# Context stage: a transposed copy of x from memory for pairs 4 to 15, the layer norm folded into the values, and deviations moved by SyncE's DMAs

## The chip, the cores and the metric

The kernel runs on one core of a Trainium2 chip. The metric is the device time of one execution in microseconds; the time before the change is the median of three executions, 522.25 us (520.49 to 522.72). Engines are named as in the profile: PE is TensorE's matmul side and PEld its weight loads, DVE is VectorE, ACT is ScalarE, POOL is GpSimd, SP is SyncE, which here only issues DMAs. A row that says SPq is the issue of a DMA.

## The reference

One layer of a perceiver: 64 sequences of 64 tokens of width 256 (x) and a context of 256 rows of width 192 for each sequence. Three residual blocks follow each other. The change touches the first (and one copy in the second).

```python
x = x + cosine(layernorm(x), ctx, Wv, bv, Wt, bt)   # this change
x = x + attention(layernorm(x), ...)                # 16 heads of 16
x = x + experts(layernorm(x), ...)                  # 14 experts, top 1

def cosine(xn, ctx, Wv, bv, Wt, bt):
    v = xn @ Wv.T + bv                              # (64, 64, 128)
    t = ctx @ Wt.T + bt                             # (64, 256, 128)
    dots = einsum('bih,bjh->bij', v, t)             # (64, 64, 256)
    return dots / maximum(norm(v)[:, :, None] * norm(t)[:, None, :], 1e-8)
```

## The kernel before

Tokens lie in SBUF in 32 tiles of 128 (`tok`). The context stage works on 16 pairs of tiles: pair n holds 256 tokens, which are 4 sequences, and the 1024 rows of their context. Three stages follow on the same engines: context (to about 113 us of the span), attention (to about 350 us) and experts. Each engine has its own instruction stream, written out in order by a `context_step`; semaphores (`need(engine, semaphore, count)`) tie them together. `run_steps` unrolls the first and last steps and makes a loop of those between.

What happens to pair n before the change:

- SP issues the load of the context, `ctxT` (768 KB, L324), and of x two pairs further (256 KB, L310). At its step 6 it first issues 12 loads of constants (L316).
- DVE takes mean and variance of x (`bn_stats`, `bn_aggr`, L601 and L609), POOL turns the variance into 1/std by a power of -0.5 (L442, L447), DVE normalises (L591), PE transposes the pair in four 128x128 transposes (L1199), and ACT copies the result out of PSUM (L1011).
- PE multiplies: the context by Wt (L1177, L1180, L1208), the transposed pair by Wv (L1191). ACT adds the biases and makes v and v squared (L1007, L1006), t and t squared (L1017, L1018).
- PE sums v squared over the 128 features (L1238), sums t squared (L1215), and multiplies v by t (L1219: the dots; L1215 and L1219 of pair n stand in PE's step n+1).
- DVE copies the sum of v squared (L629) and multiplies it by that of t squared (L622), ACT takes that product to the power -0.5 by Ln and Exp (L998, L1000), DVE multiplies by the dots (L653), POOL adds to x (L464), and DVE and POOL take the statistics of the new x for the next block (L615, L635, L453 to L460).

PE's step t holds, in this order: L1177, L1180, L1191 (pair t), L1199 (pair t+1), L1208 (pair t), L1215 and L1219 (pair t-1), L1238 (pair t). The product of `rnorm` and the dots of pair t-1 (L653) must be done before PE may overwrite the dots' bank in step t+1, so DVE, ACT and PE form a loop through `cos_sbuf`.

In the attention stage a tile's values are also needed with their halves of 64 partitions swapped: SP moves them by two DMAs a tile (`v_swap`, L356) and ACT spreads them from there (L1046, L1047).

Of the kernel before, what the change touches and what calls it, by code (L numbers as in the profile page):

```python
# [15 lines left out]
P = 128  # L16
# [7 lines left out]
NB = NT // 2  # L24
# [18 lines left out]
ZEROED, CONSTS = 4, 12  # L43
LO, HI = 8, 28
# [65 lines left out]
def build(nc, x, ctxT, wvT, wtT, xb, wqT, wkT, avT, woT, bq, bk, bv, bo, boc, woN, routerT, w1, w2, b1T, b2, out):  # L110
    routed = nc.dram_tensor("routed", ((E + 1) * REGION, REC), F32).ap()
    ctx = ExitStack()
    with ctx:
# [3 lines left out]
        def sem(name):  # L117
# [11 lines left out]
                   for n in range(2))  # L129
        pair_xn, pair_xnT = (w2_s[:, 4 * CW + 16 * SC + n * 4 * D:4 * CW + 16 * SC + (n + 1) * 4 * D]  # L130
                             .rearrange("p (s j) -> p s j", s=2) for n in range(2))

# [16 lines left out]
        xbv_s, xbt_s = xb_s[:, 0:1], xb_s[:, 1:2]  # L149
        bq_s = sb("bq_s", [P, KC])  # L150
# [24 lines left out]
        vT, vsq = (arena[:, 4096 + n * 2 * D:4096 + (n + 1) * 2 * D].rearrange("p (s j) -> p s j", s=2) for n in range(2))  # L175
        norm, rnorm, cos = (arena[:, 5120 + n * 4 * SC:5120 + (n + 1) * 4 * SC].rearrange("p (s j) -> p s j", s=2)
# [16 lines left out]
        pair_rstd = sb("pair_rstd", [P, 2, 2])  # L193
# [12 lines left out]
        v_swap = sb("v_swap", [P, 2, D])  # L206
# [65 lines left out]
        def t_bank(p, b):  # L272
# [5 lines left out]
        swap_in = [sem(f"swap_in{n}") for n in range(2)]  # L278
# [7 lines left out]
            a_stats_raw a_stats a_vareps a_rstd a_xn a_xT_psum a_xT t_psum t_sbuf v_psum v_sbuf  # L286
# [16 lines left out]
        def _(sp):  # L303
# [9 lines left out]
            def load_tokens(i, k):  # L313
# [8 lines left out]
                else:  # L322
                    need(sp, s["t_psum"], i - 3)
                    sp.dma_start(ctx_in_sb[:, k], ctxT[bass.ds(i, 1)].rearrange("o p j -> (o p) j"))\  # L324
                        .then_inc(ctx_in[k], 16)
                if paired(i + 2):
                    load_x(i + 2, (k + 2) % 4)
            run_steps(sp, load_tokens, 0, NB, 8, 12)

# [7 lines left out]
            def attention_moves(i, k):  # L337
# [14 lines left out]
                if live(i):  # L352
                    need(sp, s["val_ok"], i + 1)
                    need(sp, s["vd_ok"], i - 1)
                    for b in range(2):
                        sp.dma_start(v_swap[(1 - b) * S:(2 - b) * S, p, :], v_s[b * S:(b + 1) * S, k, :])\  # L356
                            .then_inc(swap_in[p], 16)
# [39 lines left out]
        def _(pool):  # L397
            for tile, value in ((ident, 0.0), (mhalf, -0.5), (eps, LN_EPS), (ones, 1.0)):
# [3 lines left out]
                               pattern=[[-1, P]], channel_multiplier=1).then_inc(s["first_made"], 1)  # L402

# [34 lines left out]
            def context_step(j, k):  # L438
# [26 lines left out]
                if isinstance(j, int) and -2 <= j < 6:  # L465
                    later_consts(j + 2)
# [102 lines left out]
        def _(dve):  # L569
# [13 lines left out]
            def context_step(j, k):  # L583
# [11 lines left out]
                if paired(t) and opening:  # L595
                    normalise()
# [940 lines left out]
```

## Time and profile before

| | |
|---|---|
| runs | 520.49, 522.25, 522.72 us |
| the profiled execution | 520.23 us, its span 518.3 us |
| busy: PE, DVE, ACT, POOL | 501.0, 346.2, 347.1, 240.9 us |
| granted TensorE clock | 0.994 of full over the span |
| context stage | about 0 to 113 us |

The span is what the profiler saw from the first to the last instruction of the program; about 2 us lie around it. Busy time of an engine is read against the span; where an engine is busy all the time in a stage, its own instructions are what the stage costs, and where none is, a loop of waits is.

### The profile page before, as it was taken

What the parts mean: (1) busy time and instruction counts of PE and PEld (TensorE: products, weight loads), DVE (VectorE), ACT (ScalarE), POOL (GpSimd) and SP (SyncE); (2) the same over time, 40 slices, a digit from 0 to 9 for tenths busy, and PEclk for the clock granted to TensorE, in tenths of its full rate; (3) what the DMA queues carried; (4) which work ended last, traced back from release to release, by engine and by line L of the source; (5) the groups of instructions that cost most, each with busy time, mean ns of one, the idle gap of its engine ahead of it and who ended that gap; (6) DMA issues with size and microseconds to landing.
All of it is one profiled execution on the core that took longest, in us unless ns stands there. A gap on an engine that the chain in (4) does not pass through costs nothing.

```text
span 518.3 us, 14429 instructions
## 1 busy us (share of the span) xinstructions
PE 501.0 (97%) x4324; PEld 397.7 (77%) x4325; DVE 346.2 (67%) x1054; ACT 347.1 (67%) x837; POOL 240.9 (46%) x405
## 2 busy tenths in 40 slices
PE   8999999999999999999999999899999999999993
PEld 6555555566788888888878888778989999999992
DVE  4578666647899989898998889997562333323231
ACT  3777777668988888889888888886444333343430
POOL 2366555335434545564555546551763232333332
PEclk9999999999999999999999999999999999999997
DMA  8954446101002223322332232247667666666520
GB/s 301 370 205 147 160 153 208 58 1 32 12 23 57 74 89 113 111 81 89 113 104 74 71 82 74 62 131 230 203 199 230 219 207 208 220 187 212 191 82 9
DMA packets 35617, 69.88 MB, mean 135 GB/s; under 512 B 5664, under 2 KB 23714, under 8 KB 35568
## 3 DMA queue, kind: packets, MB, share of 16 engines
q1 hardware_dynamic: 31680, 60.19, 37.2%
q0 software_dynamic: 3456, 8.85, 4.6%
q8 instruction: 22, 0.36, 0.3%
q10 hardware_dynamic: 432, 0.26, 0.2%
q14 instruction: 27, 0.22, 0.2%
HBM read 54.21 MB, written 11.60 MB: 127 GB/s over the span
## 4 chain that ended last, share of the span: by engine, by line
PE 85%; DVE 7%; issue 4%; POOL 1%; ACT 1%; DMA 1%; DVEq 0%; POOLq 0%; ACTq 0%
PE psum L1392 13%; PE psum L1405 12%; PE psum L1327 8%; PE psum L1278 6%; PE psum L1165 6%; PE psum L1286 5%; PE psum L1299 5%; PE psum L1340 4%; PE psum L1246 4%; PE psum L1208 3%; PE psum L1215 3%; PE psum L1177 3%; PE psum L1191 3%; PE psum L1219 3%; PE psum L1180 3%
## 5 line engine op out<-in xcount | busy, mean ns | idle before, releaser
L1392 PEld LDWEIGHTS psum<-arena,ring 128*128 128x128 f32 x640 | 77.3, 192 | 3.5 <-issue 1.7
L1392 PE MATMUL psum<-arena,ring 128*128 128x128 f32 x640 | 78.2, 275 | 0.9 <-ACT arena L1109 0.6
L1405 PE MATMUL psum<-w_s,arena 128*128 x320 | 76.0, 381 | 0.0
L929 DVE TENSOR_TENSOR arena<-psum,tok 128x256 f32<-128x256 f32 x40 | 17.0, 424 | 84.8 <-PE psum L1405 83.1
L1103 ACT ACTIVATE arena<-psum 128x256 f32<-128x256 f32 x40 | 15.4, 384 | 86.6 <-PE psum L1165 56.3
L1405 PEld LDWEIGHTS psum<-w_s,arena 128*128 128x128 f32 x320 | 57.8, 190 | 6.5
L490 POOL TENSOR_TENSOR ov<-o_n,v_s 128x256 f32<-128x256 f32 x32 | 23.5, 734 | 80.1 <-DVE o_n L694 80.1
L1073 ACT ACTIVATE arena<-kT,head_mask 128x256 f32<-128x256 f32 x128 | 57.4, 501 | 0.0
L545 POOL DMA_INDIRECT out<-arena,token_of x40 | 39.9, 998 | 19.9 <-POOL token_of L537 14.1
L1109 ACT ACTIVATE arena<-psum,b_s 128x128 f32<-128x128 f32 x160 | 45.4, 374 | 3.7 <-PE psum L1392 2.2
L797 DVE TENSOR_REDUCE smax<-psum 128x16 f32<-128x1024 f32 x32 | 39.0, 1218 | 2.8 <-PE psum L1299 1.6
L537 POOL TENSOR_TENSOR token_of<-slot_rec,zero_u 128x1 uint32<-128x1 uint32 x40 | 9.5, 237 | 65.2 <-DVE arena L934 65.0
L484 POOL DMA_INDIRECT routed<-rec,pos x32 | 34.0, 1063 | 8.4 <-issue 5.5
L811 DVE TENSOR_TENSOR arena<-psum,smax 128x1024 f32<-128x1024 f32 x32 | 37.6, 1176 | 0.0
L1278 PE MATMUL psum<-arena 128*64 128x34 f32 x1024 | 36.1, 225 | 0.3 <-ACT arena L1023 0.3
L1278 PEld LDWEIGHTS psum<-arena 128*64 128x64 f32 x1024 | 32.5, 138 | 4.8 <-issue 3.9
L1327 PEld LDWEIGHTS psum<-xnT,wk_s 128*128 128x128 f32 x256 | 33.2, 191 | 3.9 <-issue 1.1
L1340 PE MATMUL psum<-av_s,xnT 128*128 128x270 f32 x128 | 34.6, 392 | 0.5 <-DVE arena L811 0.5
L1299 PE MATMUL psum<-arena,qT 64*64 64x256 f32 x512 | 35.0, 389 | 0.0
L1037 ACT ACTIVATE arena<-arena 128x1024 f32<-128x1024 f32 x32 | 33.5, 1048 | 2.1 <-DVE arena L811 1.6
L1327 PE MATMUL psum<-xnT,wk_s 128*128 128x128 f32 x256 | 34.1, 276 | 0.8 <-ACT xnT L1084 0.5
L1286 PE MATMUL psum<-wo_s,oT 128*128 128x270 f32 x128 | 34.7, 393 | 0.0
(193 smaller groups left out, 1122.5 us busy)
## 6 DMA issues: line engine op xcount, KB each, us to landing
ring<-w SPq DMA_DIRECT2D x40, 512.0 KB, 3.6
w_s<-ctxT SPq DMA_DIRECT2D x15, 768.0 KB, 4.6
w_s<-w SPq DMA_DIRECT2D x16, 448.0 KB, 3.5
slot_rec<-routed SPq DMA_DIRECT2D x40, 132.0 KB, 3.3
tok<-x SPq DMA_DIRECT2D x16, 256.0 KB, 4.7
v_swap<-v_s SPq DMA_DIRECT2D x64, 64.0 KB
routed<-pad_rec SPq DMA_DIRECT2D x1, 1980.0 KB, 10.8
tok<-b SPq DMA_DIRECT2D x14, 128.0 KB, 3.3
```

Of the source, the lines that this page charges most:

```text
L545: pool.indirect_dma_start(out=out, out_offset=bass.IndirectOffsetOnAxis(ap=token_of[:, q, :], axis=0), in_=yout[:, q, :], in_offset=None, ...
L797: dve.tensor_reduce(smax[:, :], s_ps, AX.X, ALU.max).then_inc(s["smax_ok"], 1)
L811: dve.tensor_tensor(prob[:, (k - 1) % 2, :].rearrange("p (h j) -> p h j", h=NH), s_ps, smax[:, :].unsqueeze(2).broadcast_to([P, NH, S]), A ...
L1073: last = act.activation(kd[:, p, :, :, g * S:(g + 1) * S], kT[:, p, :].rearrange("p (c b j) -> p c b j", c=KC, b=2), ACT.Copy, scale=head_ ...
L1109: last = act.activation(hidT[:, p, f * P:(f + 1) * P], hid_bank(p)[:, f * P:(f + 1) * P], ACT.Gelu, bias=b1_s[:, bass.ds(e * FC + f, 1)])
L1278: mm = pe.matmul(bank(7)[h, n * VW:(n + 1) * VW], probT[:, p, n * P + b * S:n * P + (b + 1) * S], vd[:, p, b, n, :], start=True, stop=True)
L1286: mm = pe.matmul(bank(6, DX), oT[:, q, d * P:(d + 1) * P], wo_s[:, d, :], start=d == 0, stop=d == KC - 1)
L1299: mm = pe.matmul(bank(g)[h, c * HG * S:(c + 1) * HG * S], qT[r, q, c * P + b * S:c * P + (b + 1) * S], kd[r, q, c, b, :], start=True, stop ...
L1327: mm = pe.matmul(bank(4)[:, at:at + P], weight[:, d, c * P:(c + 1) * P], xnT[:, p, d * P:(d + 1) * P], start=d == 0, stop=d == KC - 1)
L1340: mm = pe.matmul(bank(6, DX), xnT[:, p, d * P:(d + 1) * P], av_s[:, d, :], start=d == 0, stop=d == KC - 1)
L1392: mm = pe.matmul(hid_bank(p)[:, f * P:(f + 1) * P], w1_s[:, r, c * F + f * P:c * F + (f + 1) * P], xgT[:, p, c * P:(c + 1) * P], start=c = ...
L1405: mm = pe.matmul(bank(2 + q, D), hidT[:, q, f * P:(f + 1) * P], w2_s[:, bass.ds(e * (FC * D) + f * D, D)], start=f == 0, stop=f == FC - 1)
```

## The change

Pairs 0 to 3 go as before. From pair 4 (`TURNED`) on, x is loaded a second time, transposed in memory on the host by layout (`xT`, 256 KB a pair), and goes raw into the product with Wv. The layer norm is applied around the product: v times std equals (x @ Wc) + std * bv, where Wc is Wv with its column mean taken off (`wvc_s`, made once from a column sum on PE), and the cosine of v needs only one factor 1/std on the dots and its square on the sum of v squared. So the bias must be multiplied by each token's std, along the free axis of the transposed values: POOL makes std for each token (`deviation`), SP stores it to memory (`deviations`, 8 bytes from each partition) and reads it back, broadcast to all partitions (`std_b`, 128 KB).

- DVE makes v (L675 of the new kernel) in place of ACT, and ACT only squares it; L653 becomes two instructions of 256 columns with a factor per token; the copy L629 becomes a product; L591 goes for pairs 4 to 15, as do the transposes and ACT's copy of them.
- The sum of v squared of pair t, which stood at the end of PE's step t, stands in step t+1 behind the product with Wv for pairs 4 to 15.
- The statistics of x are taken five pairs ahead in place of four, just ahead of the product by `rnorm`; pairs 4 and 5 are both taken in DVE's step 0.
- SP's step i now issues xT, ctxT and x, then waits for the stored deviations of pair i-1 and for a v of pair i-3, issues their broadcast, waits for POOL's deviations of pair i and stores them.
- In the attention stage `v_swap` and its DMAs go: ACT reads the other half of the partitions of `v_s` itself.

```diff
+TURNED = 4
+AHEAD = 5
@@ SP
                     need(sp, s["t_psum"], i - 3)
+                    if not isinstance(i, int) or i >= TURNED:
+                        sp.dma_start(xT_s[:, k], xT[bass.ds(i, 1)].rearrange("o p j -> (o p) j")).then_inc(ctx_in[k], 16)
                     sp.dma_start(ctx_in_sb[:, k], ctxT[bass.ds(i, 1)].rearrange("o p j -> (o p) j"))\
                         .then_inc(ctx_in[k], 16)
                 if paired(i + 2):
                     load_x(i + 2, (k + 2) % 4)
+                if not turned(i - 1):
+                    spread_deviations(i - 1, (k - 1) % 2)
+                if not turned(i):
+                    need(sp, s["a_std"], i - TURNED + 1)
+                    sp.dma_start(deviations[bass.ds(i, 1)].rearrange("o p h -> (o p) h"), pair_std[:, bass.ds(i * 2, 2)])\
+                        .then_inc(s["std_out"], 16)
+            def spread_deviations(n, q):
+                need(sp, s["std_out"], arrivals(n - TURNED, 0, 1, 16))
+                need(sp, s["v_sbuf"], n - 1)
+                sp.dma_start(std_b[:, q, :], deviations[bass.ds(n, 1)].rearrange("o p h -> o (p h)").broadcast_to([P, 2 * P]))\
+                    .then_inc(std_in[q], 16)
...
-                    need(sp, s["val_ok"], i + 1)
-                    need(sp, s["vd_ok"], i - 1)
-                    for b in range(2):
-                        sp.dma_start(v_swap[(1 - b) * S:(2 - b) * S, p, :], v_s[b * S:(b + 1) * S, k, :])\
@@ POOL, behind the sum into tok (j), in context_step
+                if isinstance(j, int) and j == 0:
+                    deviation(TURNED, 0)
+                if paired(j + AHEAD) and not (isinstance(j, int) and j < 0):
+                    deviation(j + AHEAD, 1 - p)
@@ DVE
+                if paired(v) and not (isinstance(v, int) and v < TURNED):
+                    need(dve, s["v_psum"], v + 1)
+                    need(dve, s["dots_psum"], v - 1)
+                    need(dve, std_in[p], arrivals(v - TURNED, p, 2, 16))
+                    dve.scalar_tensor_tensor(vT[:, p, :].rearrange("f (h t) -> f h t", h=2),
+                                             std_b[:, p, :].rearrange("f (t h) -> f h t", h=2), xbs_s[:, :],
+                                             bank(p, 2 * P).rearrange("f (h t) -> f h t", h=2), ALU.mult, ALU.add)\
+                        .then_inc(s["v_sbuf"], 1)
...
+                if isinstance(j, int) and j == 0:
+                    raw_statistics(TURNED, 0, 0)
+                    statistics(TURNED, 0)
+                if paired(j + AHEAD) and not opening:
+                    raw_statistics(j + AHEAD, (k + AHEAD) % 4, p)
+                    statistics(j + AHEAD, p)
@@ PE
-            for n in range(12):
+            for n in range(11):
                 pe.matmul(bank(7, P), ident[:, :], ones[:, :], start=True, stop=True)
+            for c in range(KC):
+                mm = pe.matmul(bank(2, H), ones[:, :], wv_s[:, c, :], start=c == 0, stop=c == KC - 1)
...
-                if paired(n):
+                if isinstance(n, int) and 0 <= n < TURNED:
                     need(pe, s["a_xn"], n + 1)
...
+                if paired(u) and not (isinstance(u, int) and u < TURNED):
+                    norm_of_v(u, q, q)
```

How the streams stand. First SP's, at its steps 4 and 5 (the waits are for semaphores; `w_s<-xT` is the transposed x, `deviations<-arena` the store of std). Before:

```order
L324 DMA w_s<-ctxT 128x1536 [waits t_psum]
L310 DMA tok<-x 128x2x256 [waits x_in2]
L324 DMA w_s<-ctxT 128x1536 [waits t_psum]
L310 DMA tok<-x 128x2x256 [waits x_in3]
L316 DMA wq_s<-wqT 128x512
```

Now:

```order
L339 DMA w_s<-xT 128x512 [waits t_psum]
L340 DMA w_s<-ctxT 128x1536
L324 DMA tok<-x 128x2x256 [waits x_in2]
L351 DMA deviations<-arena 128x2 [waits a_std]
L339 DMA w_s<-xT 128x512 [waits t_psum]
L340 DMA w_s<-ctxT 128x1536
L324 DMA tok<-x 128x2x256 [waits x_in3]
L357 DMA arena<-deviations 128x256 [waits v_sbuf,std_out]
L351 DMA deviations<-arena 128x2 [waits a_std]
L330 DMA wq_s<-wqT 128x512
```

Everything from pair 5's loads on, the 12 constants (the first of them is the last row) and pair 8's x among it, now stands behind a wait for `a_std`, POOL's deviations of pair 4.

Second DVE's step 3 (v of pair 4, norms of pair 3). Before:

```order
L601 BN_STATS pair_stats<-tok 128x6
L591 TENSOR_SCALAR w_s<-tok,pair_mv,pair_rstd 128x256 [waits a_xT_psum,a_rstd,a_stats_raw]
L591 TENSOR_SCALAR w_s<-tok,pair_mv,pair_rstd 128x256
L609 BN_AGGR pair_mv<-pair_stats 128x2 x2
L615 BN_STATS stats<-tok 128x6 [waits tok_sum]
L615 BN_STATS stats<-tok 128x6
L622 TENSOR_SCALAR arena<-psum,vnorm 128x256 [waits vnorm_sbuf,norms_log,dots_psum]
L622 TENSOR_SCALAR arena<-psum,vnorm 128x256
L629 COPY vnorm<-psum 128x2 [waits std_ok,stats_raw,vnorm_psum]
L635 BN_AGGR mv<-stats 128x2 [waits std_ok,stats_raw]
L635 BN_AGGR mv<-stats 128x2
L653 SCALAR_TENSOR_TENSOR arena<-arena,psum 128x512 [waits tok_sum,norms_inv]
```

Now:

```order
L675 SCALAR_TENSOR_TENSOR arena<-arena,xbs_s,psum 128x256 [waits std_in0,first_made,dots_psum,v_psum]
L691 BN_STATS stats<-tok 128x6 [waits tok_sum]
L691 BN_STATS stats<-tok 128x6
L696 BN_AGGR mv<-stats 128x2 [waits std_ok,stats_raw]
L696 BN_AGGR mv<-stats 128x2
L703 TENSOR_SCALAR arena<-psum,vnorm 128x256 [waits vnorm_sbuf,norms_log,dots_psum]
L703 TENSOR_SCALAR arena<-psum,vnorm 128x256
L649 BN_STATS pair_stats<-tok 128x6 [waits a_vareps,x_in0]
L649 BN_STATS pair_stats<-tok 128x6
L655 BN_AGGR pair_mv<-pair_stats 128x2 [waits a_stats_raw]
L655 BN_AGGR pair_mv<-pair_stats 128x2
L734 SCALAR_TENSOR_TENSOR arena<-arena,psum 128x256 [waits tok_sum,norms_inv]
```

The statistics of a later pair (here pair 8's, waiting for its x) moved from the head of the step to a place between the norms and the product by `rnorm`, and the normalising is gone.

Third PE's step 5. Before:

```order
L1177 MATMUL psum<-w_s,wt_s 128x512 [waits t_sbuf,ctx_in1]
L1180 MATMUL psum<-w_s,wt_s 128x512
L1191 MATMUL psum<-w_s,wv_s 128x256 [waits v_sbuf,vnorm_sbuf,a_xT]
L1191 MATMUL psum<-w_s,wv_s 128x256
L64 REGISTER_ALU
L1199 MATMUL psum<-ident,w_s 128x128 [waits a_xT,a_xn]
L1199 MATMUL psum<-ident,w_s 128x128 x3
L1208 MATMUL psum<-w_s,wt_s 128x512 x2
```

Now:

```order
L1276 MATMUL psum<-w_s,wt_s 128x512 [waits t_sbuf,ctx_in1]
L1279 MATMUL psum<-w_s,wt_s 128x512
L1297 MATMUL psum<-w_s,arena 128x256 [waits v_sbuf,vnorm_sbuf]
L1297 MATMUL psum<-w_s,arena 128x256
L1266 MATMUL psum<-ones,arena 128x1 [waits vsq_ok]
L1266 MATMUL psum<-ones,arena 128x1
L1319 MATMUL psum<-w_s,wt_s 128x512 x2
L1328 MATMUL psum<-w_s,ones 64x512 [waits cos_sbuf,t_sbuf]
```

The four transposes are gone, and the sum of v squared (of the pair before) stands in their place.

## Rows read from the trace of the kernel before

**Rows 1.** The page: PE's busy time, and the chain that ended last.
```profile
PE 501.0 (97%) x4324; PEld 397.7 (77%) x4325; DVE 346.2 (67%) x1054; ACT 347.1 (67%) x837; POOL 240.9 (46%) x405
PE 85%; DVE 7%; issue 4%; POOL 1%; ACT 1%; DMA 1%; DVEq 0%; POOLq 0%; ACTq 0%
```

**Rows 2.** Busy us of each engine in one pair's step; then clock, DMA.
```profile
58.48:65.07 6.59, 6.59 (x35) 3.45 (x34) 4.35 (x15) 4.70 (x7) 3.34 (x7) 1.00 0.47 171
```

**Rows 3.** Timeline: start us, us, engine, line, what; PE in pair 3's step.
```profile
24.86 0.61 PE L1238 MATMUL psum<-ones,arena 128*128 128x1 f32 x4
25.33 1.10 PE L1177 MATMUL psum<-w_s,wt_s 128*128 128x512 f32 x2
...
27.13 1.03 PE L1191 MATMUL psum<-w_s,wv_s 128*128 128x256 f32 x4
...
27.99 0.60 PE L1199 MATMUL psum<-ident,w_s 128*128 128x128 f32 x4
...
28.52 1.13 PE L1208 MATMUL psum<-w_s,wt_s 64*128 64x512 f32 x4
```

**Rows 4.** The chain in order of time, 24 to 40 us: start, us, what.
```profile
28.16 0.44 PE psum L1199 x4
```

**Rows 5.** Timeline, late in the stage: the loop of dots, norms and cosine.
```profile
89.10 1.08 PE L1215 MATMUL psum<-w_s,ones 128*64 128x512 f32 x4
...
90.01 1.03 PE L1219 MATMUL psum<-w_s,arena 128*64 128x256 f32 x8
...
93.32 0.69 DVE L653 SCALAR_TENSOR_TENSOR arena<-arena,psum 128x512 f32<-128x512 f32 x1 [1.14 <-ACT arena L1000]
...
95.69 0.20 PEld L1215 LDWEIGHTS psum<-w_s,ones 128*64 128x64 f32 x4 [0.76 <-issue]
```

**Rows 6.** Timeline, opening: pair 0's cosine and sum, PE's next dots.
```profile
19.18 0.15 DVE L629 COPY vnorm<-psum 128x2 f32<-128x2 f32 x1
...
20.62 0.69 DVE L653 SCALAR_TENSOR_TENSOR arena<-arena,psum 128x512 f32<-128x512 f32 x1 [1.29 <-ACT arena L1000]
...
21.39 1.27 POOL L464 TENSOR_TENSOR tok<-tok,arena 128x512 f32<-128x512 f32 x1 [4.55 <-DVE arena L653]
...
22.99 1.08 PE L1215 MATMUL psum<-w_s,ones 128*64 128x512 f32 x4
...
26.44 0.70 POOL L457 TENSOR_TENSOR rstd<-vareps,mhalf 128x2 f32<-128x2 f32 x1
```

**Rows 7.** Timeline: SP's issues (x, the first constant, pair 6's context).
```profile
12.17 0.43 SPq L310 DMA_DIRECT2D tok<-x  x1
...
17.37 0.47 SPq L316 DMA_DIRECT2D wq_s<-wqT  x1
...
23.76 0.43 SPq L324 DMA_DIRECT2D w_s<-ctxT  x1
```

**Rows 8.** DMAs: count, KB each, median us from issue to landing.
```profile
tok<-x SPq DMA_DIRECT2D x16, 256.0 KB, 4.7
...
routed<-rec,pos POOLq DMA_INDIRECT x32, 2.9
...
boc_s<-boc SPq DMA_DIRECT2D x1, 1.0 KB, 3.6
```

**Rows 9.** One line's instructions: ns min/median/max.
```profile
L601 DVE BATCH_NORM_STATS2 pair_stats<-tok x32: 407/414/428, 4.1 to 87.7; 128x6 f32<-128x256 f32 x32
...
L774 DVE TENSOR_TENSOR v_s<-psum,bv_s x32: 383/424/426, 115.8 to 343.5; 128x256 f32<-128x256 f32 x32
```

**Rows 10.** Timeline: DVE's normalising beside POOL's memset.
```profile
35.29 3.40 DVE L591 TENSOR_SCALAR w_s<-tok,pair_mv,pair_rstd 128x256 f32<-128x256 f32 x2
...
36.37 1.86 POOL L409 MEMSET rec<- 128x2112 f32 x1
```

**Rows 11.** Timeline: PE's warm-up products before the first pair.
```profile
1.78 5.18 PE L1161 MATMUL psum<-ones,ident 128*128 128x128 f32 x24 [1.78 <-POOL ident L401]
```

**Rows 12.** Timeline: PE at the passage to attention.
```profile
124.82 1.15 PE L1340 MATMUL psum<-av_s,xnT 128*128 128x270 f32 x4 [0.53 <-DVE arena L811]
```

More of the change, by code:

```diff
@@ L277, in build @@
         ctx_in = [sem(f"ctx_in{n}") for n in range(4)]
-        swap_in = [sem(f"swap_in{n}") for n in range(2)]
+        std_in = [sem(f"std_in{n}") for n in range(2)]
         rec_out = [sem(f"rec_out{n}") for n in range(RING)]
@@ L402, in _ @@
                                pattern=[[-1, P]], channel_multiplier=1).then_inc(s["first_made"], 1)
+            for tile, value in ((pair_rstd, LOG_SCALE ** 0.5), (pair_rvar, LOG_SCALE)):
+                pool.memset(tile[:, 0:2 * TURNED], value).then_inc(s["vnorm_unit"], 1)
             def later_consts(i):
@@ L604, in context_step @@
                     need(dve, s["a_stats_raw"], n + 1)
-                if paired(t) and not opening:
-                    normalise()
-                if paired(n):
-                    for h in range(2):
-                        whole = dve.bn_aggr(pair_mv[:, q, h, :], pair_stats[:, q, h])
-                    whole.then_inc(s["a_stats"], 1)
-                b = j - 1
+                    for h in range(2):
+                        whole = dve.bn_aggr(pair_mv[:, p, h, :], pair_stats[:, p, h])
@@ new lines, in norm_of_v @@
+                def norm_of_v(j, q, column):
+                    need(dve, s["vnorm_psum"], j + 1)
+                    need(dve, s["norms_kept"], j - 1)
+                    dve.tensor_tensor(vnorm[:, q, :], bank(column)[:, 2 * P:2 * P + 2], pair_rvar[:, bass.ds(j * 2, 2)],
+                                      ALU.mult).then_inc(s["vnorm_sbuf"], 1)
+                if paired(j) and not (isinstance(j, int) and j < TURNED):
+                    need(dve, s["a_std"], j - TURNED + 1)
+                    norm_of_v(j, q, q)
@@ L1169, in context_step, with norm_of_v @@
                 t, p, n, u, q = i, k % 2, i + 1, i - 1, (k - 1) % 2
+                def norm_of_v(v, r, column):
+                    need(pe, s["vsq_ok"], v + 1)
+                    for j in range(2):
+                        mm = pe.matmul(bank(column)[:, 2 * P + j:2 * P + j + 1], vsq[:, r, j * P:(j + 1) * P], ones[:, 0:1],
+                                       start=True, stop=True)
+                    mm.then_inc(s["vnorm_psum"], 1)
                 if paired(t):
@@ new lines, in context_step @@
+                if paired(t) and isinstance(t, int) and t < TURNED:
+                    norm_of_v(t, p, 1)
+                if isinstance(t, int) and t == NB - 3:
+                    pe.wait_ge(s["consts_in"], 16 * RESTS)
+                    pe.wait_ge(s["v_sbuf"], t + 1)
+                    for a in range(KC):
+                        mm = pe.matmul(fold[:, 0, :], ones[:, :], rt_s[:, a, :], start=a == 0, stop=a == KC - 1)
+                    mm.then_inc(s["csum_psum"], 1)
+                if isinstance(t, int) and t == NB - 2:
+                    pe.wait_ge(s["vnorm_sbuf"], t)
+                    for d in range(KC):
+                        for a in range(KC):
+                            pe.matmul(fold[:, 1 + d, :], woN_s[:, a, d * P:(d + 1) * P], av_s[:, a, D:DX], start=a == 0,
+                                      stop=a == KC - 1)
+                    for a in range(KC):
+                        mm = pe.matmul(fold[:, 3, :], ones[:, :], bor_s[:, a, :], start=a == 0, stop=a == KC - 1)
+                    mm.then_inc(s["fold_psum"], 1)
```

179 lines of the change are left out of this document (110 added, 69 removed).

## The prediction

> **What bounds the kernel.** I read the page first: PE is busy for 97% of the span and makes up 85% of the chain that ended last [rows 1]. That is an average, so I read the context stage by windows. One pair's step is 6.59 us long; PE is busy in all of it at the full clock (2.4 GHz), ACT for 4.70, DVE 4.35, POOL 3.34 us, and the DMA engines at a share of 0.47 [rows 2]. So in this stage time goes only where PE's own instructions go, as long as no loop of waits becomes longer than PE's step, and no transfer comes late.
>
> Then the loop. From the start of L1215 at 89.10 through the dots (L1219, 90.01), norms, Ln and Exp to the end of L653 (93.32 + 0.69 = 94.01) it takes 4.9 us, and PE comes back to L1215 at 95.69 [rows 5]: 1.7 us of slack.
>
> **Part 1, the transposes go (the gain).** Twelve pairs, 4 to 15, lose L1199. By starts in the timeline the four transposes take from 27.99 to 28.52, 0.53 us [rows 3]; the chain gives them 0.44 [rows 4]. I take the middle, 0.49: 12 x 0.49 = 5.9 us (5.3 to 6.4). The sum of v squared (0.47 us, 24.86 to 25.33 [rows 3]) moves and is not saved: pair 15's runs one piece later, beside attention's first products.
>
> **Part 2, the loop with the new parts.** L653 as two halves of 256 columns costs 2 x 0.42 = 0.84 in place of 0.69 (nearest: a 128x256 DVE instruction with a PSUM operand, 424 ns [rows 9]); the bounds are 0.69 and 0.85. The statistics between norms and L653 (two of 414 ns [rows 9] and two short ones, together 1.05 us) fit under the 1.3 us of Ln and Exp, which DVE idles through now (1.14 idle [rows 5]). The loop becomes 5.1 us; PE's new step is 6.59 - 0.49 = 6.10. Slack 1.0 us, so no cost. Making v on DVE (0.42) replaces L591, and DVE's sum falls; ACT loses the copy of the transposes and one evacuation. POOL gains four small instructions a pair, about 1.35 us (0.70 for the power [rows 6], the others as short as their neighbours), and stays under 5 us of 6.10. In steady state SP starts its step as PE ends L1208 of the pair four before, so xT, context and broadcast are there about a step early or more.
>
> **Part 3, the opening (the loss).** This is what the order of SP shows: behind x of pair 6 (issued 12.17 [rows 7]) SP now waits for POOL's deviations of pair 4. I follow that chain.
> - DVE: behind L629 (done 19.33 [rows 6]) come the statistics of pairs 4 and 5, 2 x 1.05 us, to 21.45; then L653 of pair 0 in halves, to 22.25, in place of 21.31. PE wants it at 22.99 [rows 6], so that delay alone costs nothing.
> - POOL: sum into tok, 1.27 [rows 6], to 23.6; the four small ones, 1.35, to 25.0. SP stores at 25.1. It has stood still for 12 us.
> - SP: issues take about 0.45 each: the store, xT, context and x of step 5 to 26.95; then it waits for the store to land. Nearest rows: 2.9 us for a DMA that writes from SBUF to memory, 3.6 for one with 8 bytes on each partition [rows 8]; I take 2.9, so 28.1. Broadcast and store of pair 5: 29.0. Twelve constants, as before 6.4 us (17.37 to 23.76 [rows 7]): 35.4. xT and context of pair 6, then x of pair 8: issued at 36.3, against 24.2 before.
> - x of pair 8 lands 4.7 us later [rows 8], with 256 KB of xT more ahead of it in the queues some 0.2 more: 41.2.
> - DVE's step 3 wants it as soon as the norms of pair 3 are done, about 38, and L653 of pair 3 is queued behind it. Statistics 1.05, L653 0.84: done 43.1.
> - PE: pair 3's step starts at 25.33 and takes 6.10, pair 4's takes 5.63 (its sum of v squared has moved to the next step), so pair 5's starts at 37.06, and its dots (of pair 4) are due 4.2 us later, 41.25. They wait to 43.2: **1.9 us lost**. Afterwards x of pair 9 (issued about 38.6, landed 43.4, wanted 46.3) is in time, and so is all that follows; SP has caught up.
>
> Bounds: if the store is no wait and DMAs are quick, x lands about 38.9 and nothing is lost; with 3.6 us for the store and a landing twice the median, the loss is 7. The nearest rows are the medians, so I stay at 1.9, with 0.8 to 3.5 as the part I believe in.
>
> Here a page bears on it. The Trainium skill, "DMA: Bandwidth & Descriptors", Specifications, says that transfers below 512 B an element are done by read and modify, and under "Anatomy of one DMA" it gives a fixed cost of about 2.0 us. By the fixed cost alone the store would be there before SP's next three issues are out, and the loss would be 1.0 us; the slower small element speaks for the 3.6 of the row, and a loss of 2.6. No row here shows such a store.
>
> **Part 4, small ones.** The column sum puts two 128x128 products in place of one of the warm-up (24 pieces, 12 products, in 5.18 us, 0.43 each [rows 11]): 0 to 0.4, since the first pair has other waits; I take 0.2. The two normalisings that took 3.40 us beside POOL's memset [rows 10] go with L591; PE had 1.7 us of slack against that, so I count 0 (0 to 0.5 gained). At the passage to attention PE waits 0.53 for DVE's chain [rows 12], and L653 in halves is in it: 0.15 lost. The swap: no copy of it waits for its DMA in the list of waits, ACT's copies stay four of the same size, and SP is on no chain there: 0. Two risks of it are that a copy across partitions is slower (cover is what ACT waits for PE in each tile) and, the other way, that 64 DMAs less do something; neither has a row. The later write of `pad_rec` has no reader before attention.
>
> **Sum.** 5.9 - 1.9 - 0.2 - 0.15 = 3.65, say 3.7. Against the profiled execution, 520.23 us (span 518.3), that is 516.5 (span 514.6). The median of the runs shown lies 2.0 above the profiled one, and since what is measured is a median too I name 522.25 - 3.7 = 518.5.
>
> **Rivals.**
> - A: the opening is hidden (x of pair 8 in time, since the queues are idle while SP stands still, and a DMA then lands faster than the median, which was taken among full queues). Gain 5.6 us: 516.7. For it: the queues would be empty when SP wakes at 25. Against: the twelve constants alone hold the issue back to 36, and DVE wants it at 38.
> - B: the opening costs two steps: the broadcast of pair 4 comes late too (wanted 34, SP issues it at 28 behind 1.3 MB), or x lands after 44. A loss of 4.5 to 5 us, gain about 1: 521.3. For it: every one of these sits in one queue of SP; against: the landings would have to be 3 us over the median.
> - C, slower: the round trip of std through memory sets the pace. SP may not issue a broadcast before the store has landed, and the next pair's loads stand behind that. SP's cycle is 0.88 us plus the store's landing; it decides from a landing of 5.2 us on. At 7 us (between the median of x and what full queues make of it) the cycle is 7.9, 1.8 over PE's 6.1; over 11 pairs 20 us, of which SP's lead hides about 9. With the 5.9 gained the kernel is some 5 us slower: 527. For it: the store stands behind 1.4 MB of loads a step, and is a write of tiny elements. Against: the DMA share of 0.47 becomes about 0.65, no more, and medians are 2.9 and 3.6.
> - D: the loop through DVE and ACT is longer than I think (v on DVE delays ACT's square, then t, then Ln). From 1.0 us more on it eats the gain; at 1.5 more the step is back at 6.6 and the time at 522.
>
> **Chances.** Forecast 0.56, A 0.17, B 0.12, C 0.08, D 0.07. What a measurement can tell from no change is 0.5%, 2.6 us: below 519.6 is faster. The forecast lies there with about nine tenths of its chance, A wholly: faster 0.68. B and D and the rest of the forecast: same 0.22. C and the tails of B: slower 0.10. The range runs from A's low side, 515.0, to B, 521.5.
>
> **What would show it.** Right: in steps 7 to 13 the start-to-start distance of PE's L1276 is 6.0 to 6.15 with PE busy throughout; one gap of 1 to 3 us before the dots of PE's step 5 (about 41 to 43 us), with DVE waiting for `tok<-x` before L649; SP standing still from about 13 to 25. Wrong: a step over 6.3, with the releaser of L1328 or L675 naming the loop or the broadcast (D, C); no gap at 41 (A); gaps in two or more steps (B). Attention's and experts' stages should be as long as before, to 0.3 us each.

## The result: slower by 1.6%, and the profile after

| | before | after |
|---|---|---|
| median | 521.37 us (519.88 to 522.72, 4 runs) | 529.98 us (527.93 to 530.85, 4 runs) |
| ratio, 95% interval | | 1.0159 (1.0134 to 1.0183) |
| profiled execution, its span | 520.23, 518.3 us | 530.85, 528.8 us |
| granted clock over the span | 0.994 | 0.981 |
| attention's first product (L1340, now L1451) starts at | 114.65 us | 124.81 us |

The last row says where the time went. I take the start of attention's first product as the end of the context stage. It comes 10.2 us later and the span is 10.5 longer, so attention and experts are as long as before to 0.3 us and nearly everything lies in the context stage. I use this mark for all experiments below. It flatters every changed kernel by up to 0.5 us: the sum of v squared of pair 15, which stood ahead of the mark, now starts behind it (L1266 at 125.94). The four runs of the kernel before have a median 0.9 us under the 522.25 from which the forecast was taken.

The page of the changed kernel, its part on busy time and its chain, answers to [rows 1]:

```profile
PE 499.4 (94%) x4278; PEld 395.6 (75%) x4279; DVE 340.4 (64%) x1059; ACT 335.4 (63%) x814; POOL 245.0 (46%) x431
...
PE 62%; DMA 15%; issue 8%; DVE 7%; POOL 4%; ACT 1%; SPq 1%; DVEq 0%; POOLq 0%; ACTq 0%
DMA deviations<-arena 14%; PE psum L1503 12%; PE psum L1516 12%; PE psum L1438 8%; PE psum L1389 6%; PE psum L1257 6%; PE psum L1397 5%; PE psum L1410 5%; PE psum L1357 4%; PE psum L1451 4%; POOL tok L509 1%; DMA arena<-deviations 1%; POOL out L594 1%; DVE o_f L862 1%; DVE arena L893 1%
```

PE does less work (499.4 against 501.0 us) and is on the chain for 62% in place of 85%. A DMA of 1 KB, the store of the deviations, is now 14% of the chain.

PE's timeline from pair 4's step on answers to [rows 3, 5]; the brackets hold PE's idle time before a row and what ended it:

```profile
36.53 1.08 PE L1328 MATMUL psum<-w_s,ones 128*64 128x512 f32 x4 [0.80 <-DVE arena L734]
37.41 1.06 PE L1332 MATMUL psum<-w_s,arena 128*64 128x256 f32 x8
38.41 1.12 PE L1276 MATMUL psum<-w_s,wt_s 128*128 128x512 f32 x2
...
41.52 1.13 PE L1319 MATMUL psum<-w_s,wt_s 64*128 64x512 f32 x4
49.87 1.98 PE L1328 MATMUL psum<-w_s,ones 128*64 128x512 f32 x4 [7.22 <-DVE arena L734]
51.60 1.95 PE L1332 MATMUL psum<-w_s,arena 128*64 128x256 f32 x8
53.48 1.48 PE L1276 MATMUL psum<-w_s,wt_s 128*128 128x512 f32 x2
...
59.89 1.13 PE L1276 MATMUL psum<-w_s,wt_s 128*128 128x512 f32 x2
...
65.94 1.13 PE L1276 MATMUL psum<-w_s,wt_s 128*128 128x512 f32 x2
...
77.35 1.08 PE L1328 MATMUL psum<-w_s,ones 128*64 128x512 f32 x4 [1.12 <-DVE arena L734]
...
85.90 1.97 PE L1328 MATMUL psum<-w_s,ones 128*64 128x512 f32 x4 [2.43 <-DVE arena L734]
```

Two things are to be seen. An undisturbed step is 65.94 - 59.89 = 6.05 us, so the saving is there. And there are four gaps, together 11.6 us, the large one at 42.6 to 49.87, with every one released by L734, DVE's product by `rnorm`. Behind the gaps of 7.22 and 2.43 us the same products take 1.98 in place of 1.08 us: PE's granted clock was at 0.50, the lower of its two levels (1.2 in place of 2.4 GHz), as the windows there show in their third number from the end:

```profile
50.00:53.00 3.00, 3.00 (x12) 1.25 (x12) 1.19 (x6) 2.42 (x3) 2.75 (x7) 0.50 0.90 82
86.00:89.00 3.00, 3.00 (x12) 1.25 (x12) 1.21 (x6) 2.42 (x3) 2.75 (x8) 0.50 0.79 215
```

From 49.87 to the product with Wv at 55.66 is 5.79 us, where an undisturbed step needs 3.7; behind the second it is 6.54. That is 2.1 and 2.9 us more. The gaps of 0.80 and 1.12 us had no such effect. So 16.6 us lost against 12 x 0.54 = 6.5 gained: 10.1 us.

What DVE waited for ahead of L734, from its timeline and from the list of waits in 12 to 110 us (total, times, longest):

```profile
47.94 0.75 DVE L649 BATCH_NORM_STATS2 pair_stats<-tok 128x6 f32<-128x256 f32 x2 [8.36 <-DMA tok<-x]
48.72 0.25 DVE L655 BATCH_NORM_AGGREGATE pair_mv<-pair_stats 128x2 f32<-128x6 f32 x2
48.89 0.84 DVE L734 SCALAR_TENSOR_TENSOR arena<-arena,psum 128x256 f32<-128x256 f32 x2
```
```profile
DVE pair_stats L649 <- DMA tok<-x: 15.7, 5, 8.4
...
DVE arena L675 <- DMA arena<-deviations: 5.8, 3, 2.6
```

DVE stands before the statistics of pair 8, whose x is not there, and L734 of pair 3 is queued behind them. SP's timeline tells why x is late; it answers to [rows 7]:

```profile
13.01 0.43 SPq L324 DMA_DIRECT2D tok<-x  x1
25.17 0.34 SPq L351 DMA_DIRECT2D deviations<-arena  x1
...
29.82 0.65 SPq L330 DMA_DIRECT2D wq_s<-wqT  x1
...
38.17 0.43 SPq L324 DMA_DIRECT2D tok<-x  x1
38.71 0.51 SPq L357 DMA_DIRECT2D arena<-deviations  x1
39.27 0.50 SPq L351 DMA_DIRECT2D deviations<-arena  x1
39.81 0.73 SPq L339 DMA_DIRECT2D w_s<-xT  x1
40.58 0.55 SPq L340 DMA_DIRECT2D w_s<-ctxT  x1
41.17 0.51 SPq L324 DMA_DIRECT2D tok<-x  x1
48.34 0.33 SPq L357 DMA_DIRECT2D arena<-deviations  x1
```

SP stands still from 13.4 to 25.17, then issues pair 8's x at 38.17, and that x is there only at 47.9, 9.8 us later. After the store at 39.27 SP may not issue the next broadcast before 48.34, since it waits for that store to land. Such waits held SP 11 times, for 55.2 us in total. The chain of waits (start, us, what) goes from store to store:

```profile
39.27 9.06 DMA deviations<-arena
...
48.71 7.27 DMA deviations<-arena
...
56.37 7.56 DMA deviations<-arena
```

The page's section on DMAs (count, KB each, median us from issue to landing) answers to [rows 8]:

```profile
w_s<-ctxT SPq DMA_DIRECT2D x15, 768.0 KB, 8.5
...
tok<-x SPq DMA_DIRECT2D x16, 256.0 KB, 8.5
```

Every load became slow, x from 4.7 to 8.5 us. What does it: the place of the store and its waits in SP's queue, or the store itself?

### The profile page after: what moved, and what is told of

The parts are those of the page before. It is cut to its first block, busy times and chain, and to the rows that moved or that the text cites. A ratio compares the mean times of both kernels' runs of the same rounds, so it can differ in the third digit from the quotient of the medians.

```text
span 528.8 us, 14236 instructions
## 1 busy us (share of the span) xinstructions
PE 499.4 (94%) x4278; PEld 395.6 (75%) x4279; DVE 340.4 (64%) x1059; ACT 335.4 (63%) x814; POOL 245.0 (46%) x431
## 4 chain that ended last, share of the span: by engine, by line
PE 62%; DMA 15%; issue 8%; DVE 7%; POOL 4%; ACT 1%; SPq 1%; DVEq 0%; POOLq 0%; ACTq 0%
DMA deviations<-arena 14%; PE psum L1503 12%; PE psum L1516 12%; PE psum L1438 8%; PE psum L1389 6%; PE psum L1257 6%; PE psum L1397 5%; PE psum L1410 5%; PE psum L1357 4%; PE psum L1451 4%; POOL tok L509 1%; DMA arena<-deviations 1%; POOL out L594 1%; DVE o_f L862 1%; DVE arena L893 1%
## 5 line engine op out<-in xcount | busy, mean ns | idle before, releaser
L594 POOL DMA_INDIRECT out<-arena,token_of x40 | 40.0, 999 | 19.5 <-POOL token_of L586 14.2
L509 POOL TENSOR_TENSOR tok<-tok,arena 128x512 f32<-128x512 f32 x16 | 20.4, 1278 | 48.3 <-DVE arena L734 48.3
L1451 PE MATMUL psum<-av_s,xnT 128*128 128x270 f32 x128 | 34.6, 392 | 0.7 <-DVE arena L893 0.7
```

What stands on the lines that cost most here:

```text
L594: pool.indirect_dma_start(out=out, out_offset=bass.IndirectOffsetOnAxis(ap=token_of[:, q, :], axis=0), in_=yout[:, q, :], in_offset=None, ...
L1451: mm = pe.matmul(bank(6, DX), xnT[:, p, d * P:(d + 1) * P], av_s[:, d, :], start=d == 0, stop=d == KC - 1)
```

## The experiments

Each ratio is against the kernel before on the same chip. The chips differ: on those of the first and third group the kernel before took 535.64 and 536.34 us, on the others 521.04 and 521.35. On the two slower chips the ratios come out 2.6 to 4.4 us better than the context stage explains; there is no trace of the kernel before from such a chip, and the reason stays open. So I compare kernels by the start of attention's first product, which no later stage touches (before 114.65, after 124.81). It is read from one execution: e8, whose context stage is that of the kernel before, has it 0.8 us later, and is behind by as much from its first product with Wv on (10.05 against 9.23 us), so differences under 1 us say nothing. Between kernels with gaps even more is open, some 3 to 4 us: the runs of e6 go from 532.44 to 539.15 us and its trace is of the slowest, and the trace of e4 is of a run of 539.64, its median 536.78. "Share" is the mean busy share of the DMA engines in 20 to 60 us, then in 62 to 92 us. It has to be read with the bytes: in 20 to 60 us the changed kernel moved 184 GB/s and e1 259.

| run | ratio (95%) | first product of attention | share |
|---|---|---|---|
| before | | 114.65 | 0.58, 0.56 |
| after | 1.0159 (1.0134 to 1.0183) | 124.81 | 0.78, 0.79 |
| e1, no trip | 0.9811 (0.9767 to 0.9856) | 107.76 | 0.74, 0.66 |
| e2, broadcast only | 0.9845 (0.9789 to 0.9900) | 107.80 | 0.85, 0.56 |
| e3, store only | 1.0017 (0.9986 to 1.0048) | 119.34 | 0.74, 0.94 |
| e4, both, no wait for the store | 1.0039 (1.0008 to 1.0070) | 118.34 | 0.82, 0.94 |
| e5, constants first | 1.0111 (1.0070 to 1.0151) | 118.44 | 0.89, 0.84 |
| e6, broadcast a step later | 1.0234 (1.0205 to 1.0263) | 131.48 | 0.71, 0.82 |
| e7, both orders | 1.0089 (1.0062 to 1.0116) | 119.69 | 0.88, 0.85 |
| e8, swap alone | 0.9998 (0.9983 to 1.0014) | 115.47 | 0.60, 0.53 |
| e9, narrow stores, no wait | 0.9824 (0.9776 to 0.9873) | 108.23 | 0.96, 0.81 |
| e10, wide stores, no wait | 0.9817 (0.9773 to 0.9861) | 107.61 | 0.78, 0.65 |
| e11, turned rows, both orders, first store later | 0.9849 (0.9817 to 0.9881) | 109.15 | 0.73, 0.57 |
| e12, turned rows alone | 0.9969 (0.9948 to 0.9989) | 112.78 | 0.77, 0.67 |

### Group 1: take the trip apart

The first run leaves out the whole trip of std through memory (the factor is 1.0), the others give back one DMA or both:

```diff
 e1: spread_deviations, the store and DVE's wait for std_in go; std_b is set to 1.0
 e2: the broadcast stays, but reads bv; no store
-                need(sp, s["std_out"], arrivals(n - TURNED, 0, 1, 16))
 e3: the store stays, with its wait for a_std; no broadcast
 e4: both stay, the broadcast reads bv and does not wait for std_out
```

> The changed kernel without the trip of std through memory: no store, no broadcast, no wait for them in SyncE's queue; std is taken as 1 in the bias (the output differs). Theory W (SyncE's wait for the store's landing paces the loads) and theory C (the two small DMAs fill the DMA engines and slow every load) both expect about 516 to 518 us, no gap of PE at step 5, x landing about 5 us. Theory X (the transposed load by itself, 256 KB more a pair, makes the landings long) expects landings of 8 us still, and 522 or more.

> As the changed kernel, without the store; the broadcast of 128 KB stays, but reads a constant row of 1 KB that lies in memory, so SyncE waits for no store (the bias gets wrong factors). W expects 516 to 518 us. C, if the broadcast is what fills the DMA engines, expects 522 or more with a median landing of x near 8 us; if it is the store, under 518 and about 5 us.

> As the changed kernel, with the store of 8 bytes a partition (and SyncE's wait for POOL before it) but without the broadcast and without the wait for the store's landing; std is taken as 1. W expects at most the opening's gap, 517 to 520 us. C, if the store is what fills the engines, expects landings of x near 8 us and 522 or more.

> Both small DMAs stay, but the broadcast reads the constant row, so SyncE never waits for a store to land (the bias gets wrong factors). The run that tells the two apart: W expects 517 to 520 us, the opening's wait for POOL alone being left, and landings back near 5 us; C expects what the changed kernel has, 526 to 530 us, with landings of 8 us.

Measured: without the trip there is no gap, the steps from 37 to 86 us are 6.05 us each, and the context stage ends 6.9 us before that of the kernel before. The arithmetic of the change gives all it was meant to, and by this mark some more. The broadcast costs no time (107.80), though context and x land in 6.7 and 6.8 us in place of e1's 5.7 and 5.9. The store with its wait for POOL costs 11.6 us (119.34), nearly all of it in one place of PE's timeline of e3, with the products behind it at the lower clock:

```profile
51.05 1.97 PE L1326 MATMUL psum<-w_s,ones 128*64 128x512 f32 x4 [8.17 <-DVE arena L732]
```

The steps after it are 6.05 us without a gap, in e4 too. So the wait of each broadcast for its store (after against e4) is worth about 6.5 us, and the opening some 11. In e3 and e4 nothing waits for a store, and still context and x land in 8.0 to 8.5 us: the slow landings do not come from those waits. Nor do they come from the 256 KB of xT a pair, which e1 loads too.

### Group 2: reorder SP's queue

```diff
 e5: the 12 constants in SP's step 4, ahead of the wait for a_std
-                if isinstance(i, int) and i == 6:
+                if isinstance(i, int) and i == 4:      (moved behind load_x)
 e6: the broadcast one step of SP later; one semaphore for even, one for odd stores
-                if not turned(i - 1):
-                    spread_deviations(i - 1, (k - 1) % 2)
+                if not turned(i - 2):
+                    spread_deviations(i - 2, k % 2)
 e7: both
 e8: the kernel before, only v_swap and its DMAs gone
-                        sp.dma_start(v_swap[(1 - b) * S:(2 - b) * S, p, :], v_s[b * S:(b + 1) * S, k, :])\
```

> The changed kernel with one thing moved: the 12 loads of constants are issued in SyncE's step 4, ahead of its wait for POOL's deviations of pair 4, in place of step 6. If the gap of PE before the dots of its step 5 (7.2 us, and 2 us of slow clock behind it) comes from the constants' issues and bytes between that wait and x of pair 8, the gap is under 2 us and the later gaps (1.1 and 2.4 us) stay, since SyncE still waits for each store to land: 8 us less than the changed kernel. If the gap comes from the store's landing in the queue alone, it stays over 5 us.

> The changed kernel with the broadcast of a pair's std issued one SyncE step later (two semaphores for the stores), so that the store has a whole step to land and nothing waits behind it. The serial wait, as the cause of the later gaps, expects steps 6 to 13 all at 6.05 us, and the opening's gap unchanged or 1 us less: 5 to 7 us less than the changed kernel. If the stores' use of the DMA engines causes the later gaps, they stay.

> Both moves together: constants ahead of the wait for POOL, and the broadcast a step later. If the two orders in SyncE's queue are the whole loss, the context stage is 5 to 7 us shorter than before the change and the time some 1 to 1.3 percent below the kernel before. If engine time of the stores matters by itself, gaps of 1 us or more remain and the time is about that of before.

> The kernel before with one part of the change alone: ACT reads the other half of the partitions of v_s itself, and v_swap and its 64 DMAs go. Expected: the same within 0.2 percent, since no instruction waited for the swap and ACT's four copies keep their size; ACT's copies across partitions 300 to 320 ns as before. The other theory, that a copy across partitions is slower or that SyncE's freed queue changes the loads of w2, expects a difference over 0.3 percent.

Measured: e5 takes the large gap away, and gaps of 0.3 to 2.0 us come in its place all over the stage, so that it ends 6.4 us before the changed kernel's (2.5 by the ratios) where I had expected 8. e6 was expected to win 5 to 7 us and made things worse: the broadcast of pair 4 now came behind the constants, and PE waited 9.96 us for the v that needs it:

```profile
51.46 2.05 PE L1299 MATMUL psum<-w_s,arena 128*128 128x256 f32 x4 [9.96 <-DVE arena L677]
```

With both orders (e7) four gaps of 1.3 to 2.2 us were left, ctxT landed in 8.6, x in 8.7 us. The orders had been mended and the loads were as slow as ever, so something else slowed them. The swap (e8) is worth nothing to within 0.2 percent, as predicted.

### Group 3: the store by itself

In e9 and e10 SP waits neither for POOL nor for a store, and there is no broadcast. Only twelve stores are added to e1, from a tensor that is there from the start. They differ in width:

```diff
-                    need(sp, s["a_std"], i - TURNED + 1)
-                    sp.dma_start(deviations[bass.ds(i, 1)].rearrange("o p h -> (o p) h"), pair_std[:, bass.ds(i * 2, 2)])\
+                    sp.dma_start(deviations[bass.ds(i, 1)].rearrange("o p h -> (o p) h"), wt_s[:, 0, 0:2])\      (e9: 128 x 8 B)
+                    sp.dma_start(deviations[bass.ds(i, 1)].rearrange("o p h -> (o p) h"), wt_s[:, 0, 0:128])\    (e10: 128 x 512 B)
```

e11 keeps the whole change and makes the elements of the store few. POOL writes std into column 0 of two 32-column blocks, VectorE turns each 32x32 block, and then partitions 0, 32, 64 and 96 hold 64 values each: 8 elements of 128 B. Constants and broadcast stand as in e7, and one thing more was moved: the store of pair 4 goes out in SP's step 5, together with that of pair 5. So SP issues pair 5's loads ahead of its first wait, at 19.5 to 20.6 us, where e7 has them at 25.5.

```diff
+                    dve.transpose(std_r[:, r, :], std_n[:, r, :]).then_inc(s["std_turned"], 1)
...
-                    sp.dma_start(deviations[bass.ds(i, 1)].rearrange("o p h -> (o p) h"), pair_std[:, bass.ds(i * 2, 2)])\
+                        sp.dma_start(deviations[bass.ds(n, 1)].rearrange("o h (b r) -> (o b) h r", b=4),
+                                     std_r[0:P:32, r, :].rearrange("b (h r) -> b h r", h=2)).then_inc(std_outs[r], 16)
```

> Leaves out the deviations: the added term is 1.0 times the bias, and each of the 12 stores sends 128 elements of 8 bytes taken from the projection weights, which are there from the start. So SP waits for nothing of POOL, there is no broadcast, and the constants keep their place. Left of the change's trip are the twelve stores alone. Theory (the stores take the DMA engines): the landings stay long, ctxT about 7.8 us and tok<-x about 8.3 us as in the run with the store only, the engines' share in 62:92 us stays near 93% against 66% with the broadcast alone; since x and ctxT are again issued at their own time, the gap of 8.2 us in the opening shrinks to 0 to 3 us, ratio 0.985 to 0.995. Rival (SP's stand for POOL, with the constants behind it, made both the landings and the gap): landings of 5.3 and 5.5 us as without any trip, share 56%, no gap, ratio 0.980 to 0.984.

> As the run with the narrow stores alone, but each store sends 128 elements of 512 bytes (64 KB instead of 1 KB). If a store costs by the number of its elements, landings and engine share are those of the narrow stores or a little more (64 KB more per pair at the 171 GB/s of the step before are 0.4 us of all engines), ratio the same within 0.3%. If it is the smallness of the element that costs, the share in 62:92 us falls from above 90% to about 60 to 65%, ctxT lands in about 5.5 to 6.2 us and x in 5.5 to 6.4 us, although 64 times as many bytes are stored.

> The whole change with the deviations made right, but VectorE turns them first in 32x32 blocks, so that four partitions hold 64 values each and a store is 8 elements of 128 bytes instead of 128 of 8; constants ahead of the waits, broadcast one step of SP later than the store. Theory (the narrow elements take the engines): landings as in the run with broadcast alone, ctxT about 6.2 us, x 6.4 us, broadcast 3.4 us, share in 62:92 us about 66%; steps of 6.05 us with no gap above 1 us; ratio 0.984 to 0.992 (the run with broadcast alone gave 0.9845), so faster than both kernels. Its own new price is 12 turnings on VectorE, between 0.2 and 0.5 us each, beside a loop that has room. Rival (a trip through memory costs by its waits, whatever its elements): gaps of 1 to 2 us in most steps as in the run with both orders changed, ratio 1.005 to 1.012.

Measured, 0 to 110 us by windows (the last three columns are PE's clock, DMA share, GB/s), for e1, e9 and e10 in this order:

```profile
0.00:110.00 110.00, 108.08 (x522) 60.22 (x525) 66.49 (x236) 66.55 (x97) 59.38 (x159) 1.00 0.63 218
```
```profile
0.00:110.00 110.00, 108.22 (x520) 60.89 (x523) 66.16 (x234) 66.08 (x96) 58.92 (x159) 1.00 0.77 218
```
```profile
0.00:110.00 110.00, 107.85 (x522) 59.79 (x525) 66.50 (x236) 66.77 (x97) 59.69 (x159) 1.00 0.64 225
```

The same bytes a second need 0.63 of the DMA engines' time without stores and 0.77 with the narrow ones. All twelve stores fall into these 110 us: 0.14 x 110 / 12 = 1.3 us of all 16 engines for 1 KB. In 62 to 92 us, with five stores and the bytes allowed for, it comes to 1.1. (The share there was 0.81 and not 0.93 as expected.) In e10 the share rises by 0.01; its own 128 packets of 27 ns make 0.2 us of all 16 engines for a store of 64 KB.

The packet records of the traces say in whose packets this time lies. The narrow store's own packets take 9 ns each, less than 0.1 us of all engines for 128 of them. Nearly all that is added lies in packets of the loads beside it: the 1920 packets of 6144 B with which the context comes take 31.3 us of all engines in e1 and 43.5 in e9. Most of them take 234 ns in both, but the longest in 20 to 92 us went from 1.6 to 5.0 us. What holds up these few is not shown.

The landings follow, first e9, then e10:

```profile
w_s<-ctxT SPq DMA_DIRECT2D x15, 768.0 KB, 8.1
...
tok<-x SPq DMA_DIRECT2D x16, 256.0 KB, 8.7
...
deviations<-wt_s SPq DMA_DIRECT2D x12, 1.0 KB, 9.4
```
```profile
w_s<-ctxT SPq DMA_DIRECT2D x15, 768.0 KB, 5.9
...
tok<-x SPq DMA_DIRECT2D x16, 256.0 KB, 5.7
...
deviations<-wt_s SPq DMA_DIRECT2D x12, 64.0 KB, 5.1
```

So neither the number of elements nor the bytes is enough by itself: it takes elements as narrow as 8 B. Two things go with that width in these runs and were not tried apart from it. In e9 the elements lie side by side in 1 KB of memory, in e10 512 B apart; and e11 below has wider elements and fewer of them at once. And yet e9 is as fast as e1 (108.23 against 107.76; I had expected up to 3 us of gap): slow landings alone cost nothing as long as SP issues its loads in time. The narrow stores by themselves cost 0.5 us, which is nothing at this accuracy. They cost much when SP is held back as well, until the slack of its loads is used up. What an SP held back costs by itself, e12 shows below.

e11 bears that out from the other side. Its landings are no longer than those of a kernel without the store, and the turning is short:

```profile
w_s<-ctxT SPq DMA_DIRECT2D x15, 768.0 KB, 4.8
...
tok<-x SPq DMA_DIRECT2D x16, 256.0 KB, 5.0
...
arena<-deviations SPq DMA_DIRECT2D x12, 128.0 KB, 4.5
```
```profile
L709 DVE STREAM_TRANSPOSE arena<-arena x12: 245/246/246, 24.8 to 87.8; 128x64 f32<-128x64 f32 x12
```

In 20 to 60 us PE is busy for 39.66 of 40 us. Its ratio, 0.9849 (0.9817 to 0.9881), beats both kernels. It comes from one of the slower chips; by the context stage alone (109.15 against 114.65) the gain is 5.5 us, about 1 percent. SP's list of waits in e11 shows how little a wait says by itself:

```profile
SPq L355 <- DVE arena L709: 41.6, 12, 4.1
```

SP waits in all twelve steps, 41.6 us in total, and it costs nothing, since PE has no gap of over 0.2 us in the stage.

### Group 4: the fourth corner

e12 is the changed kernel with the turned rows and nothing else; constants and broadcast keep the places of the change.

> The changed kernel with nothing altered but the stores: the deviations are turned on VectorE and stored as 8 elements of 128 bytes, while constants and broadcast keep the places of the change (constants at SP's step 6, behind the wait for pair 4's deviations; each broadcast behind the wait for its store). It fills the fourth corner of a table: narrow elements with the change's order 1.0159, narrow with both orders mended 1.0089, wide with both mended 0.9849. Theory (the elements are the larger cause, SP's long stand the smaller, and the waits for a store of few elements are short): SP still stands from 13.4 to about 26 us and then issues the constants, x of pair 8 goes out near 38 us but lands in about 5 us instead of 9.8, so one gap of 2 to 4 us stays in the opening, the later steps are 6.05 us without gaps, stores land in 2 to 3.5 us; ratio 0.990 to 0.998. Rival (the wait for each store's landing sets SP's cycle whatever its elements): gaps of 1 to 2.5 us come back every few steps as in the changed kernel, ratio 1.005 to 1.015. Second rival (the orders were worth nothing once elements are wide): no gap above 1 us, ratio 0.983 to 0.988.

Measured: one gap, as the theory had it, where x of pair 8 is late (issued 36.13, there at 43.1, 7.0 us), and the products behind it at the lower clock:

```profile
45.08 1.97 PE L1342 MATMUL psum<-w_s,ones 128*64 128x512 f32 x4 [2.88 <-DVE arena L748]
```

That makes a table of four, by the start of attention's first product (before: 114.65):

| | the change's order | both orders mended |
|---|---|---|
| 128 elements of 8 B | 124.81 | 119.69 |
| 8 elements of 128 B | 112.78 | 109.15 |

The elements are worth 12.0 and 10.5 us, the orders 5.1 and 3.6. These are single executions, and the lower right corner holds the later store of pair 4 too, so the second number of each is of two things. Three of the corners ran on chips of like speed, and their ratios give 9.9 us for the elements (after against e12) and 3.6 for the orders (after against e7). With few elements the change is a gain even in its own order, 0.9969 (0.9948 to 0.9989); with many it is a loss in both.

## Why the prediction was wrong

The time was outside the range and on the other side. What happened is rival C, which had a chance of 0.08, joined by a fault in the opening that B described (x of pair 8 landed at 47.9, B had "after 44") and by a cost that no case held: what the stores do to the loads.

- **Part 1 was right.** A step went from 6.59 to 6.05 us, 0.54 where I took 0.49.
- **Part 2 was right in its sizes.** L734's halves take 0.84, v on DVE (L675) 0.47 against 0.42, and neither DVE, ACT nor POOL set the pace: e1 has no gap. Its sentence "xT, context and broadcast are there about a step early or more" was wrong. It assumed that SP starts each step when PE lets it; SP started when the last store had landed.
- **Part 3 had the mechanism and missed the size; this is the step that failed.** SP stood still from 13.4 to 25.17 (predicted 25.1), issued pair 8's x at 38.17 (36.3), and DVE's statistics held back L734 and PE's dots, all as described. The term that was mis-sized is the landing of x, 9.8 us in place of 4.9. Its issue was 1.9 us later than forecast too, and PE's dots were due 1.4 later, so the gap was 7.2 us and not 1.9. The lower clock behind it, a term that the sum did not have, added 2.1. The 4.7 us of [rows 8] was measured with the engines at a share of 0.47 (in one step) and no narrow stores. I used it for a kernel that adds such stores.
- **"SP has caught up" was wrong.** I put the store at 2.9 us, the median of a DMA that POOL issues and that moves 1 KB from each partition, and said that C decides from 5.2 us on. It took 3.5 to 9.4, median near 7. The sentence against C was "the DMA share of 0.47 becomes about 0.65, no more". It counted bytes, and by bytes it holds: e1 has 0.66 in 62 to 92 us. The stores took it to 0.94 in e3. SP went from store to store in 7.7 to 9.4 us (39.27, 48.71, 56.37, 64.33, 73.33), as C's sum has it for such landings, in place of PE's 6.05.
- **The rule that I had cited pointed the right way.** I had set the Trainium skill, "DMA: Bandwidth & Descriptors", Specifications (under 512 B the DMA engines read and modify) against the fixed cost of about 2.0 us in the same page. The rows side with the first in this much: small elements are slow, since 64 times the bytes in elements of 512 B took a sixth of the engines' time. That a read and modify is the cause, no run here shows. I had priced it for the store's own landing only, 3.6 in place of 2.9 us; what it costs is the engines' time, which all loads pay. The Trainium skill gives no figure for that; e9 does. Its fixed cost stands under the path of GpSimd, and SyncE issues this store; no store of std landed under 3.0 us in any run.
- **Part 4** was right within its small terms, the column sum by luck if at all. The swap measured 0. The first product with Wv starts 0.36 us later (9.59 against 9.23), where I took 0.2 for the column sum, but only 0.04 of it is there when the first transposes start (7.05 against 7.01). The rest comes at L1279, which waited 0.89 us for context. e8 has no column sum, and its first product with Wv starts at 10.05, behind a wait of the same kind.

In the sum: gain 5.9 was 6.9 (e1), of which up to 0.5 is pair 15's sum that now stands behind the mark. The loss of 1.9 was about 17: the change's order costs 5.0 with few elements (e12 against e1), and the narrow elements add 12 on top of it. Without that order they cost 0.5 (e9 against e1).

What stays open: what holds up the loads' packets beside a narrow store, and whether it is the width of the elements or their lying side by side in memory; the 3 us on the slower chips; and the 1.4 us between e11 and e1 (e11's steps are 6.15 us in place of 6.05 in the middle of the stage; which instruction sets that was not tried).

## What to carry to other kernels

Price a small DMA by its elements as well as by its bytes and its landing, and charge it to the loads beside it: 128 elements of 8 bytes added over 1 us of busy time to every DMA engine here. A landing read in a trace holds for that trace's traffic; when a change adds such a DMA, forecast with a landing twice as long (here 4.7 became 8.5 us), and see which wait it reaches. A wait on an issuing queue is harmless until the loads behind it lose their lead, so write down for each load how early it is, and let neither a first-time wait nor a batch of constants stand ahead of the one with the least lead.

## What the hardware showed

- A store of 128 elements of 8 B to memory adds 1.1 to 1.3 us of busy time on all 16 DMA engines (e9 against e1), and the context and x beside it land in 8.1 and 8.7 us in place of 5.7 and 5.9. The store's own packets take 9 ns each; the time lies in a few long packets of the loads. With elements of 512 B a store takes 0.2 us (e10). With 8 elements of 128 B nothing could be seen (e11).
- Behind gaps of PE of 2.43, 2.88, 7.08, 7.22, 8.17 and 9.96 us the next products ran at the lower clock (1.98 in place of 1.08 us for L1328). Behind gaps of 2.04 (e5 and e7), 2.12 (e6) and 2.23 us (e7) the first group of products took its usual time and a later one was slow: in e7 the product after L1330 took 1.79 in place of 1.03 us, with a granted clock of 0.50 in 90 to 92 us. Gaps of 0.3 to 1.53 us that stood alone brought nothing of the kind. So in this kernel a gap of 2 us or more cost itself and a second part of 1.4 (e12) to 3.8 us (e6).
- VectorE turns 128x64 numbers in 32x32 blocks in 246 ns (e11). ACT's copies from the other half of the partitions of `v_s` take 317 and 311 ns, those within a half 298 and 314 (e8).
